# Routing in two parts and the first expert tile prepared before the last attention chunk, in a one-core attention and mixture-of-experts kernel

## The reference

```
h = layernorm(x) * (1 + ca) + sa
q, k = relu(h Wq + bq), relu(h Wk + bk);  v = h Wv + bv
s = gamma*s + k v^T;  z = gamma*z + k;  attn = (q s) / (q.z + eps)     # over time
x = x + ga * attn
h = layernorm(x) * (1 + cb) + sb
expert = argmax(h Wr^T + br)                                            # 8 experts
x = x + gb * (relu(h W1[expert]^T + b1[expert]) W2[expert]^T + b2[expert])
```

## Time and profile before

| | us |
|---|---|
| median of three runs | 453.95 |
| range of the three | 453.8 to 455.54 |
| the profiled execution | 455.38 |
| its span in the trace | 453.3 |

### The profile page before, as it was taken

How to read it: one execution, slowest core, us unless ns; L and a number is a source line. 1 busy time by engine, 2 the same in 40 slices (tenths; PEclk the granted TensorE clock), 3 DMA queues, 4 the chain that set the end, 5 groups by cost and what they waited for, 6 DMA issues and landing times.

```text
span 453.3 us, 14515 instructions
## 1 busy us (share of the span) xinstructions
PE 427.4 (94%) x4729; PEld 383.4 (85%) x4729; DVE 373.5 (82%) x1006; ACT 336.1 (74%) x853; POOL 260.5 (57%) x427
## 2 busy tenths in 40 slices
PE   6999899999999999958799999999999999999993
PEld 3988788898898888834379999999999999999992
DVE  2877999999999999889768877787777777788863
ACT  1557789899999998948177777777777777777770
POOL 2032577777767777674555666666666666664332
PEclk9999999999999999998899999999999999999997
DMA  8724455555555674120141212222221222100000
GB/s 279 263 94 140 149 176 163 169 162 165 163 165 169 179 247 142 48 82 23 48 122 48 72 52 73 70 70 70 65 71 56 71 64 65 51 26 25 21 18 2
DMA packets 23447, 46.90 MB, mean 103 GB/s; under 512 B 4683, under 2 KB 17228, under 8 KB 21200
## 3 DMA queue, kind: packets, MB, share of 16 engines
q1 hardware_dynamic: 17424, 31.82, 21.9%
q0 software_dynamic: 4992, 12.60, 9.3%
q10 hardware_dynamic: 960, 1.57, 1.0%
HBM read 35.22 MB, written 13.50 MB: 107 GB/s over the span
## 4 chain that ended last, share of the span: by engine, by line
PE 52%; DVE 36%; issue 6%; DMA 2%; ACT 2%; POOL 1%; DVEq 0%; ACTq 0%; POOLq 0%
PE ps_o L1583 22%; PE ps_va L1562 11%; PE ps_qk L1562 11%; DVE w L966 5%; DVE arena L1074 4%; DVE arena L1067 3%; DVE st L1077 2%; DVE arena L1101 2%; DVE arena L865 2%; PE ps_k L1300 2%; DMA w<-in_wmod 2%; DVE logits L1090 2%; DVE arena L1059 2%; DVE st L778 1%; DVE arena L1095 1%
## 5 line engine op out<-in xcount | busy, mean ns | idle before, releaser
L1583 PE MATMUL ps_o<-w,arena 128*128 x912 | 106.0, 273 | 0.2 <-issue 0.2
L1583 PEld LDWEIGHTS ps_o<-w,arena 128*128 128x128 f16 x912 | 87.5, 98 | 10.1 <-issue 0.5
L1215 DVE COPY w<-w 128x2048 f16 x78 | 60.9, 782 | 31.7 <-PE ps_qk L1562 29.0
L702 ACT ACTIVATE arena<-ps_qk,arena 128x128 f32<-128x128 f32 x156 | 44.5, 368 | 47.0 <-PE ps_qk L1562 47.0
L558 POOL DMA_INDIRECT out_rows<-arena,slot_token x39 | 46.2, 1185 | 33.8 <-POOL arena L552 30.7
L1201 DVE TENSOR_TENSOR arena<-arena 128x512 f16<-128x512 f32 x78 | 53.7, 688 | 10.1 <-ACT arena L710 9.9
L1562 PE MATMUL ps_qk<-arena,w 128*128 128x128 f16 x936 | 58.6, 219 | 0.6 <-DVE w L1215 0.6
L1562 PE MATMUL ps_va<-arena,w 128*128 128x128 f16 x936 | 58.6, 219 | 0.2 <-ACT arena L702 0.2
L552 POOL TENSOR_TENSOR arena<-arena 128x256 f32<-128x256 f32 x38 | 27.5, 722 | 51.8 <-DVE arena L1289 51.8
L1562 PEld LDWEIGHTS ps_qk<-arena,w 128*128 128x128 f16 x936 | 55.4, 98 | 2.0 <-issue 0.8
L1562 PEld LDWEIGHTS ps_va<-arena,w 128*128 128x128 f16 x936 | 55.4, 98 | 0.8 <-DVE w L1215 0.4
(11 more groups left out here) (230 smaller groups left out, 867.6 us busy)
## 6 DMA issues: line engine op xcount, KB each, us to landing
w<-in_w_raw SPq DMA_DIRECT2D x16, 1024.0 KB, 5.4
token_rows<-arena SPq DMA_DIRECT2D x64, 128.0 KB, 2.6
arena<-in_x SPq DMA_DIRECT2D x32, 128.0 KB, 2.3
b_sb<-in_b2b SPq DMA_DIRECT2D x1, 1024.0 KB, 5.6
w<-in_wmod ACTq DMA_DIRECT2D x1, 768.0 KB, 8.6
w<-in_wqkv SPq DMA_DIRECT2D x1, 768.0 KB, 8.3
arena<-token_rows,slot_token POOLq DMA_INDIRECT x39, 3.5
out_rows<-arena,slot_token POOLq DMA_INDIRECT x39, 2.7
```

The source lines that it names most:

```text
L702: last = act.activation(hid[:, f, :], bank[("qk", "va")[h]][:, (f % 4) * P:(f % 4 + 1) * P], ACT.Relu, bias=consts_now[:, r, f:f + 1], sca ...
L1215: dve.tensor_copy(now[:, :, i * F // 2:(i + 1) * F // 2], of[:, :, i * F // 2:(i + 1) * F // 2]).then_inc(s_w1, 1)
L1583: last = pe.matmul(bank[f"o{n % 2}"][:, 0:D], hid_parts[:, r % 2, b, f, :], w[:, bass.ds(m, 1), a, f * D:(f + 1) * D].rearrange("p a d -> ...
```

## The change

The routing is done in two parts. The chunks of the first half (NA = 16, both sequences) are routed alone, during attention slots 21 to 29; of their tokens exactly TA = 9 full tiles are formed (16 chunks of 128 tokens over eight experts always fill at least nine). These are tiles 0 to 8. All tokens left over, and the second half, make the other TB = 30 tiles, whose routing runs beside the first expert tiles. NT stays 39. The rows in DRAM are laid out anew (`row_of`), so that the first half lies in rows 0 to 2047, and the host puts input and output in that order. In detail:

- VectorE gets 28 instructions in slots 21 to 29 (`early_route_1`, `_2`, `_3`), the eight-column ones and some of 63 to 144 columns; the picking of chunks 8 to 15 moves within slots 21 to 25. TensorE gets two count matmuls in slot 22 and 16 number matmuls of nine columns at the end of slot 31. GpSimd writes the 16 one-hot matrices, four in each of slots 28 to 31 (`mark_slots`).
- ScalarE's high pieces of the last matrix move into slots 32 and 33. VectorE's low pieces of the matrix before it all come in slot 32, with the tokens of the early tiles (`early_tokens`). At the start of slot 33, ahead of chunk 31's residual, VectorE runs `first_tile`: four low pieces of the last matrix, both copies of tile 0's first matrix, and tile 0's low part of the tokens.
- GpSimd gathers tiles 0 and 1 in slot 33 after the second normalisation of chunk 29, and tiles 2 and 3 after that of chunk 31.
- In the expert part VectorE does `late_ranks` (5 instructions) in slot 0, `late_places` (4) in slot 1, `late_slots` (8) in slot 2, `late_matrices` (3) in slot 3 and `late_tokens` (7) at the start of slot 6. GpSimd gathers nothing in slots 3, 4 and 5; it multiplies `in_tile` (960 columns) and writes 24 one-hot matrices there, eight a slot, of 128 columns. ScalarE writes the last eight. TensorE runs the 32 number matmuls of 30 columns after tile 4's second matrix (`late_numbers`).
- Of the 57 matmuls on zeros between attention and experts (30 and 27) 8 stay (4 and 4).

```diff
+            def mark_slots(of, numbers, i):
+
+                for n in range(i * MARKS, (i + 1) * MARKS):
+                    last = pool.tensor_scalar(of[:, n, :], slot_no16, numbers[:, n:n + 1], None, ALU.is_equal)
+                last.then_inc(s_bits, 1)
...
+                if (k, u) == (NCH // B, 1):
+                    first_gathers()
+                    tile_constants()
+
             slots(pool, *ATT, slot)
...
+            pool.wait_ge(s_x1, NCH)
+            for n in range(2, 4):
+                gather(n)
+                constants_of(n)
...
+            for s in range(NT + 1):
+                for n in gathered_in(s):
+                    if n == TA:
+                        pool.wait_ge(s_tokens, 2)
+                    gather(n)
...
+                if TA - 6 <= s < TA - 3:
+                    i = s - TA + 6
+                    if i == 0:
+                        pool.wait_ge(s_minus, 2)
+                        pool.wait_ge(s_hot, 2)
+                        pool.tensor_tensor(in_tile, in_tile, code16.unsqueeze(2).to_broadcast([P, NCH, TB]),
+                                           ALU.mult).then_inc(s_numbers, 1)
+                    mark_slots(in_slot, slot_f, 2 * i)
+                    mark_slots(in_slot, slot_f, 2 * i + 1)
...
+            def slot(k, u):
+                if (k, u) == (FULL + 1, 0):
+                    token_hi(0, 0)
...
+                if (k, u) == (FULL, 1):
+                    first_tile()
...
+            def first_tile():
+
+                for i in range(PIECES):
+                    lo_piece(NM + i // 2, 1 - i // 2, i % 2, last=True)
+                dve.wait_ge(s_wlo, NM)
+                dve.wait_ge(s_b2, 16)
+                level()
+                m = matrix_number(0)
+                copy_w1(m, 0, 0)
+                copy_w1(m, 0, 1)
+                token_lo(0, 0)
...
+                    if n == 0:
+                        late_ranks()
+                        pe.wait_ge(s_gb_sb, 1)
...
+                    if n == TA - 5:
+                        late_numbers()
```

More of the change, by code:

```diff
@@ L65, with row_of, in_rows, from_rows @@
 B1_AT = GB_AT + DK * B
+def row_of(g, r):
+    half = NCH // B // 2
+    return ((r if g < half else 3 - r) * half + g % half) * P
+def in_rows(a):
+    half = S // 2
+    return np.concatenate([a[0, :half], a[1, :half], a[1, half:], a[0, half:]])
+def from_rows(a):
+    half = S // 2
+    return np.stack([np.concatenate([a[:half], a[3 * half:]]), a[half:3 * half]])
 def constants():
@@ new lines, in build @@
+        code_f = place[:, 216:216 + TB]
+        in_tile = rows_1[:, 0:NCH * TB // 2].bitcast(F16).rearrange("p (n t) -> p n t", t=TB)
+        count_i, full_i, full, upto_tile, first = (pick[:, i * NE:(i + 1) * NE] for i in range(5))
+        pos, pos_i, tile_i, slot_i = (pick[:, 40 + i * NCH:40 + (i + 1) * NCH] for i in range(4))
+        slot_f, tile_16 = pick[:, 168:168 + NCH], pick[:, 200:200 + NCH // 2].bitcast(F16)
+        tile_f, token_f, empty_f = (pick[:, 216 + i * TB:216 + (i + 1) * TB] for i in range(3))
@@ L560, in slot @@
                                             oob_is_err=False).then_inc(s_out[n % 4], 16)
-            slots(pool, *FFN, slot)
             for r in range(4):
@@ new lines, in late_places @@
+            def late_places():
+                level()
+                hop(dve.tensor_tensor_scan(upto_tile, con("ones")[:, 0:1].to_broadcast([P, NE]), full, float(TA),
+                                           ALU.mult, ALU.add))
+                hop(dve.tensor_tensor(first, upto_tile, full, ALU.subtract))
+                hop(dve.scalar_tensor_tensor(of_experts(place), by_expert(first, NCH), float(P), of_experts(place),
+                                             ALU.mult, ALU.add))
+                dve.wait_ge(s_chosen, 2)
+                mark(dve.tensor_tensor(place, place, chosen16, ALU.mult))
@@ L1290, in slot @@
                                       ALU.mult).then_inc(s_ys, 1)
+                    if n == 0:
+                        late_places()
+                    if n == 1:
+                        late_slots()
+                    if n == 2:
+                        late_matrices()
             slots(dve, *FFN, slot)
```

504 lines of the change are left out of this document (319 added, 185 removed).

## The result

The changed kernel takes **470.6 us** (median of 4 runs, 470.34 to 472.13) beside 453.88 for the kernel before (453.69 to 455.54) on the same chip: a ratio of 1.0367, 95% interval 1.0334 to 1.04. The forecast was 459.2 with a range up to 464.0: the direction was right, the size was not. The profiled execution has a span of 468.8 us, 15.5 more than the 453.3 of before. The medians differ by 16.7, because the traced execution of before (455.38) was 1.5 us above its median and the traced one of the changed kernel (470.63) was not.

What follows compares the result with a forecast made beforehand. TensorE or VectorE was taken to bound each stage: both without slack in attention, TensorE full in the expert tiles. -1.6 + 2.4 + 3.5 + 0.9 = +5.2 us on the median of 453.95 gives 459.2, range 450.5 to 464.

Steps and rivals of the forecast that it cites:

- Step 1: Attention slots 21 to 29: VectorE's 28 added instructions delay what follows by 4.4 us, bounds 2.5 and 6.5.
- E: The delay from VectorE's 28 added instructions in attention slots 21 to 29: 4.4 us, bounds 2.5 and 6.5.
- step 2: Attention's end to tile 0: tile 0 starts at 213.2 before adding E; VectorE idles 4 us at its low token part.
- step 3: Tile 0 to tile 1: gather 2 stands behind chunk 31; tile 1 starts at 230.3 against 231.88, -1.6 us.
- Step 4: Expert slots 0 to 3: VectorE's late parts cost 6.9 us against 4.4 of slack; +2.4 us, bounds 0.5 and 4.
- Step 5: Late numbers: TensorE waits for GpSimd's 24 one-hot matrices at 0.30 us each; +3.5 us, +1.5 at 0.216, +6 at 0.41.
- Step 6: What is left: gathers of tiles 9 and 10 +0.3, TensorE's low clock from tile 1 +0.6; together +0.9 us.
- The clock and GpSimd cost more: Rival: contention takes E to 6.5, a matrix to 0.41, TensorE's clock falls again; +12 us, 463 to 467, chance 0.13.
- the three signs of a wrong prediction: Tile 1 starting below 227, a one-hot matrix under 0.2 us, or slots 1 to 4 keeping to 5.52 us each.

Runs made afterwards that it cites:

- The run with two columns: The changed kernel, but GpSimd writes only two of the 128 columns of each of its 24 late one-hot matrices: 461.86 us, ratio 1.0173 to the kernel before.

## Why the prediction was right and wrong, step by step

**Step 1, right.** VectorE's slot 32 starts at 202.27, where before it started at 198.06: 4.2 us later, forecast 4.4. The mechanism holds as well: from slot 21 to slot 32 VectorE was busy 58.85 us instead of 54.62, which is the whole delay, and 3.8 of it had come by slot 29.

**Steps 2 and 3, right mechanism, too small a gain.** Forecast, with E: tile 0 at 217.6, tile 1 at 230.3. Measured: 217.45 and 228.20. The idle times are where step 2 put them (VectorE's timeline):

```profile
206.80 4.01 DVE L1072 SCALAR_TENSOR_TENSOR w<-w,w_scale 128x512 f16<-128x512 f32 x4 [0.85 <-ACT w L700]
211.87 1.29 DVE L1417 COPY w<-w 128x2048 f16 x2 [1.06 <-issue]
215.65 0.48 DVE L1456 SCALAR_TENSOR_TENSOR arena<-ps_x,small,arena 128x256 f16<-128x256 f32 x1 [2.48 <-ACT arena L706]
216.50 0.49 DVE L1278 SCALAR_TENSOR_TENSOR arena<-ps_o,den,arena 128x264 f32<-128x264 f32 x1
```

The one ahead of tile 0's low token part was 2.5 us and not 4. Tile 0's agreement is partly luck: its tokens were ready at 216.1, and what held TensorE until 217.45 were the six matmuls on zeros ahead of the tile (214.89, 2.77 us at a clock of 0.50). The 6.94 us taken over from before held matmuls on zeros too. VectorE, which waits for the tokens alone, came to chunk 31 at 216.0 and not 217.5, and from gather 2's start (223.51) to TensorE's transposes it was 3.8, where I had added 1.1 of issue to the 3.5 of landing, which already holds it. So tile 1 gained 3.7 and not 1.6. That chunk 31 stands behind tile 0's block was right; the runs showed the second hold-up on GpSimd that step 3 missed.

**Step 4, too small.** +2.4 forecast with 4 as the upper bound, 5.7 measured, with the waits for `copy_w1` that the step named (1.96 us in slot 4, 0.94 in slot 5). Slots 1 to 3, where GpSimd had no matrix to write, cost 1.7 of it; slots 4 and 5, beside the product and the matrices, cost 4.0. The bound left out that this work would stretch what stands beside it: 2.52 for an instruction of 0.47. With the product on VectorE these two slots took 2.9 us less.

**Step 5, the step that failed.** "One of 128 columns is not in the trace ... I take 0.30, between the ends, as one input is read and not two." It is 0.604 alone and 0.785 there. The other terms of the sum hold: product 1.8 (1.9), adding and scattering 5.5 (5.8); the 24 matrices took 18.6 where the prediction has 7.2. So the last one was ready at L + 26.8 and not L + 14.9 (L, the end of `late_slots`, was 246.5). TensorE came later too, at L + 15.9 and not L + 11.8, by what slots 4 and 5 had lost, and so the step cost 11.3 instead of 3.5. Against the forecast of +5.2 the spans show +15.4, a miss of 10.2: step 5 missed by 7.8, step 4 by 3.3, step 6 by 1.2, and step 3 by 2.1 the other way. (On the medians the miss is 11.4; the rest is the traced execution of before, which stood above its median.) The upper bound was wrong too: it scaled the slope of a two-input product, and the one-input form is steeper, 2.5 against 1.65 ns a column. The run with two columns is the test of the step: at 0.43 a matrix the numbers took 4.4 us, between its +3.5 and +6, and the kernel 461.9, inside the range on record. By the spans it stands at +6.6 against the forecast's +5.2, the rest being step 4's, step 6's and step 5's own 0.9, less what step 3 gained.
The Trainium skill (GPSIMD Engine Reference, 4.1 Engine selection) calls one-input work roughly line-rate, which gave the estimate of 0.11 us for 128 columns. The measurement decides against it: 2.5 ns a column, 0.604 in all. The Trainium skill (GPSIMD Engine Reference, Specifications) names contention with VectorE's instructions with two SBUF inputs; the product on VectorE (2.52 to 0.59) agrees. GpSimd's own matrices, with one input each, were held up beside VectorE as well, up to 1.0 us for two columns.

**Step 6.** Tile 1 did start at the lower level, as forecast: its first half took 2.35 us from start to start instead of 1.34. Against before that cost almost nothing, since before's slot 1 took 6.36 us and this one 6.53. The larger cost, +2.1 at slot 6 where +0.6 was forecast in all, came behind a wait that step 5 had made too short. The late gathers cost nothing where they stood, and cost 6 to 7 us when I moved them.

**The rivals.** "The clock and GpSimd cost more" had two of its three parts right, the dearer matrix and the clock that falls once more, and a chance of 0.13; its first part, E at 6.5, did not come (4.2). Its 463 to 467 rested on the same bound of 0.41. None of the three signs of a wrong prediction came up: they watched for a matrix under 0.2 us, and none watched for one over 0.41.

## What to carry to other kernels

An operation that the trace doesn't hold is a measurement to make or a range to keep open: scale from the same form or not at all, and when 24 of them stand in one queue, the bound should come from the dearest neighbour. Work moved to an engine with 40% idle time is not free when the two engines hold each other up, as GpSimd and VectorE did here (0.47 to 2.52 us, 0.60 to 1.76): count what it stretches as well. And when a hold-up is taken away, look for the second one in the next engine's queue: here the one on VectorE was worth 1.2 us alone and 4.6 with the one on GpSimd behind it. The one on GpSimd alone was not tried.
